# Reordering the feed-forward steps of slots 0 and 1 in a software-pipelined local-attention and feed-forward stage

## The reference, cut to what matters

```python
def local_attention(q, k, v):        # 16 heads of 64, windows of 32 that look one window back
    ...
    sim = jnp.where(mask, -jnp.finfo(sim.dtype).max, sim)
    attn = jax.nn.softmax(sim, -1)
    out = jnp.einsum('bhwij,bhwje->bhwie', attn, bv2)
...
def attn_layer(x, Wqkv, qs, ksc, Wo):
    ...
    q = l2norm(q) * qs
    k = l2norm(k) * ksc
    q = q * cos * scale + rotate_half(q) * sin * scale
    ...
    return out @ Wo
def ffn_layer(x, g, bln, W1, b1, W2, b2):
    xn = (x - mu) / jnp.sqrt(var + 1e-05) * g + bln
    hg = xn @ W1 + b1
    a, gate = jnp.split(hg, 2, -1)
    return a * jax.nn.gelu(gate, approximate=False) @ W2 + b2
for i in range(DEPTH):               # DEPTH = 6
    x = attn_layer(shift_tokens(x), ...) + x
    x = ffn_layer(shift_tokens(x), ...) + x
```

## Time and profile before

| | |
|---|---|
| median of three runs | 2726.36 us |
| the profiled execution's own time | 2725.75 us |
| its span, first to last instruction | 2723.9 us |
| mean granted TensorE clock | 0.926 of full |
| PE busy | 2409.4 us, 88% of the span |
| DVE busy | 1616.5 us, 59% |
| ACT busy | 1235.0 us, 45% |
| POOL busy | 1033.6 us, 38% |
| the stage's part of the span | about 753 to 1911 us |
| in 861 to 1885 us (1024 us): PE, DVE, ACT, POOL busy | 967.5, 826.2, 681.1, 798.4 us |
| granted clock in 861 to 1885 us | 1.00 |

### The profile page before, as it was taken

How to read it: one execution, slowest core, us unless ns; L and a number is a source line. 1 busy time by engine, 2 the same in 40 slices (tenths; PEclk the granted TensorE clock), 3 DMA queues, 4 the chain that set the end, 5 groups by cost and what they waited for, 6 DMA issues and landing times. The chain is left out here.

```text
span 2723.9 us, 46399 instructions
## 1 busy us (share of the span) xinstructions
PE 2409.4 (88%) x16011; PEld 1423.7 (52%) x16011; DVE 1616.5 (59%) x3815; ACT 1235.0 (45%) x3220; POOL 1033.6 (38%) x901
## 2 busy tenths in 40 slices
PE   5989998699679999999999999998698996996998
PEld 2446666355435555565656556565356443554443
DVE  3544544475378887888788878885463213573233
ACT  1324452155246666666666666665151111362221
POOL 2010000101188877777777878774100002000000
PEclk7989998798789999999999999999796897797999
DMA  1110000000010000000000000000000000000010
GB/s 59 25 27 1 1 1 1 16 3 2 13 39 5 21 17 14 13 17 25 9 10 25 9 14 21 14 4 1 16 3 16 23 23 12 13 2 24 23 35 19
DMA packets 45344, 41.97 MB, mean 15 GB/s; under 512 B 7421, under 2 KB 35749, under 8 KB 45108
## 3 DMA queue, kind: packets, MB, share of 16 engines
q1 hardware_dynamic: 42612, 36.59, 4.6%
q10 hardware_dynamic: 2496, 2.36, 0.4%
HBM read 33.36 MB, written 0.52 MB: 12 GB/s over the span
## 5 line engine op out<-in xcount | busy, mean ns | idle before, releaser
L3286 POOL TENSOR_TENSOR l1fb_p<-l1fb_p,l1fb_rden 128x640 f32<-128x640 f32 x192 | 240.4, 1252 | 218.6 <-DVE l1fb_rden L3353 218.6
L3278 POOL TENSOR_TENSOR l1fb_rinv<-l1fb_ssq,neghalf 128x8 f32<-128x8 f32 x192 | 319.1, 1662 | 8.5 <-DVE l1fb_ssq L3343 8.4
L3482 PE MATMUL ps<-l1fb_wqkv,l1fb_xs 128*128 128x512 f32 x576 | 298.3, 628 | 9.1 <-DVE l1fb_xs L3309 4.3
L3438 ACT ACTIVATE l1fb_p<-ps,l1fb_shift 128x128 f32<-128x128 f32 (+1 forms) x768 | 282.6, 392 | 0.3
L3280 POOL TENSOR_TENSOR l1fb_qk<-l1fb_qk,l1fb_rinv 128x512 f32<-128x512 f32 x192 | 206.6, 1076 | 15.0
L3445 ACT ACTIVATE l1fb_pT<-ps 128x512 f32<-128x512 f32 x192 | 114.7, 597 | 191.8 <-PE ps L3534 191.8
L3419 ACT ACTIVATE l1fb_sq<-ps 128x512 f32<-128x512 f32 x192 | 114.9, 598 | 169.8 <-PE ps L3482 166.0
L3348 DVE TENSOR_REDUCE l1fb_shift<-ps 128x4 f32<-128x640 f32 x192 | 157.1, 818 | 50.9 <-PE ps L3512 48.9
L3438 ACT ACTIVATION_READ_ACCUMULATOR l1fb_p<-ps,l1fb_shift 128x1 f32 x768 | 168.2, 219 | 0.0
L3534 PE MATMUL ps<-ident,l1fb_p 128*128 128x128 f32 x768 | 125.8, 286 | 41.0 <-ACT l1fb_g L3454 28.6
L3512 PE MATMUL ps<-l1fb_kT,l1fb_qT 64*128 64x128 f32 (+1 forms) x1536 | 147.3, 310 | 0.0
(11 more groups left out here) (708 smaller groups left out, 5425.6 us busy)
## 6 DMA issues: line engine op xcount, KB each, us to landing
l1fb_wqkv<-in_L_ffn_Wqkv SPq DMA_DIRECT2D x24, 256.0 KB, 2.7
l3f_w<-in_L_ffn_W SPq DMA_DIRECT2D x21, 256.0 KB, 3.1
l2f_w<-in_L_ffn_W SPq DMA_DIRECT2D x16, 256.0 KB, 3.1
l1fb_wqkv<-in_L_ffn_Wqkv SPq DMA_DIRECT2D x6, 512.0 KB, 4.1
l1fb_wo<-in_L_ffn_Wo SPq DMA_DIRECT2D x6, 512.0 KB, 4.3
l1fb_w<-in_L_ffn_W SPq DMA_DIRECT2D x6, 341.0 KB, 2.9
l1fb_w<-in_L_ffn_W SPq DMA_DIRECT2D x6, 128.0 KB
x_tok<-in_x SPq DMA_DIRECT2D x1, 512.0 KB
```

The lines of the kernel that those rows point to most:

```text
L3278: nc.gpsimd.tensor_tensor(w.rinv[:, u, :], w.ssq[:, u, :], chip.neghalf[:, 0:8], ALU.pow).then_inc(*w.unit_norm.end(f"rinv{u}"))
L3286: nc.gpsimd.tensor_tensor(p, p, w.rden[:, c, :, :].rearrange("p j q -> p (j q)").unsqueeze(2).to_broadcast([P, 2 * QT, SEEN]), ALU.mult)\
L3438: last = nc.scalar.activation(w.p[:, c % 4, j, q, 0:hi - lo], ps[:, SCORE_BANK(c) + j, lo:hi], ACT.Exp, bias=w.shift[:, c, j, q:q + 1], ac ...
L3482: nc.tensor.matmul(ps[:, PROJ_BANK(u), :], w.xs[:, x.odd, q * P:(q + 1) * P], w.wqkv[:, col:col + 512], start=True, stop=True)\
```

## The change

Three of the four strings change; no step is added or taken away, and every wait stays as it is. In slots 0 and 1 TensorE's queue has `gate2'` ahead of `V6'` and `value2'` ahead of `V7'`. ScalarE's queue has the three gelus ahead of the exponentials `X0`. VectorE's queue has `inv0` behind `att6'` and `max1` in place of ahead of them, and `g2'` ahead of the rotation `r0`. GpSimd's string stays.

```diff
-PE_PLAN = """S0 T6' t4' gate01' V6' gate2'    S1 T7' t5' p0 value01' V7' value2' p1    S2 T0 t6' y2' V0 p2    S3 T1 t7' y1 V1 p3
+PE_PLAN = """S0 T6' t4' gate01' gate2' V6'    S1 T7' t5' p0 value01' value2' V7' p1    S2 T0 t6' y2' V0 p2    S3 T1 t7' y1 V1 p3
...
-DVE_PLAN = """inv7' att5' max0 edge6' r7' tab    inv0 att6' max1 edge7' g0' g1' r0 g2'  inv1 att7' max2 edge0 x2' r1  inv2 att0 max3 edge1 r2 x1
+DVE_PLAN = """inv7' att5' max0 edge6' r7' tab    att6' max1 inv0 edge7' g0' g1' g2' r0  inv1 att7' max2 edge0 x2' r1  inv2 att0 max3 edge1 r2 x1
...
-ACT_PLAN = """c6' e4' X0 gelu0' gelu1' gelu2'    c7' e5' q0 X1 q1    c0 e6' X2 q2    c1 e7' X3 q3
+ACT_PLAN = """c6' e4' gelu0' gelu1' gelu2' X0    c7' e5' q0 X1 q1    c0 e6' X2 q2    c1 e7' X3 q3
```

## The result

The changed kernel takes **2735.21 us** (median of seven runs, 2730.09 to 2740.71) against 2726.36 before (seven runs, 2724.94 to 2728.76). The ratio is 1.0034, with a 95% interval from 1.0023 to 1.0045: slower by a third of a per cent. The forecast was 2730.2, within 0.2%; its range, 2722 to 2737.5, holds the time. The mechanism came as forecast, the sum was too small: +3.8 against +8.9. I had named the change "the same", with 5.5 us as the bound; by that bound it is slower, for which I had given 0.24.

The account below looks back on a forecast made before the run. The prediction took TensorE's idle gaps in `l1_ffn` as the bound. Its terms, +2.1 us for 21 units and +1.7 for the others, made +3.8 on 2726.36: 2730.2 us, range 2722 to 2737.5.

Parts of the forecast that it names:

- The waits: TensorE, each unit: waits of T7' and T0 go, 1.97 us; waits of 0.94 (value2') and 1.13 (t6') come.
- ScalarE's chain: ScalarE: load, gelus, second load, X0 ending at 963.40, then c7' and e5'; value2' starts at 964.42, waiting 0.94.
- rival 2: ScalarE ahead of gelu0': table load waits for the gates, +0.37 us a unit, 2735.9 us; chance 0.10.
- Behind `value2'` on TensorE: TensorE: value2', V7', p1 and S2 take 3.39 us, so T0 is reached at 967.81 and t6' at 968.30.
- The collision: Slot 1: GpSimd's n7' product gets the port ahead of VectorE's clamp; t6' at 969.43, without a lock 968.96.
- Rivals 1 and 3: Port: 1, VectorE's clamp first, -0.17 a unit, 2724.5, chance 0.14; 3, no collision, -0.37 a unit, 2720.3, chance 0.06.
- Rival 4: GpSimd's power also holds the port, delaying VectorE's addition: +0.51 us a unit, 2738.8 us; chance 0.03.
- Rival 5: TensorE: both old waits go and nothing replaces them, -1.97 us a unit, 2686.7 us; chance 0.03.
- the wait for `g2'`: TensorE at T0: this wait goes; had it been alone, it was worth 0.6 us.
- the +0.10 a unit: t6' on TensorE moves from 969.33 to 969.43 in each repeating unit; times 21, +2.1 us.
- Single units: Units outside the repeating pattern: unit 0 +0.85, unit 23 +1.54, unit 24 about -0.74 us; together +1.7.
- my own case: The forecast itself, +3.8 us to 2730.2 us, called the same; chance 0.58, with 0.08 for exceeding 5.5 us.

Follow-up runs that it names:

- e5: Changed kernel with GpSimd's n7' ahead of s0 and VectorE's tab moved from ahead of att6' to behind max1: 2715.22 us.
- e2: Changed kernel with VectorE's g2' put back behind the rotation r0: 2723.72 us.
- e7: Kernel before with the gelus ahead of X0, inv0 behind max1, n7' ahead of s0 and tab behind max1: 2710.01 us.
- e3: Kernel before with only TensorE's new order and g2' ahead of r0; ScalarE and inv0 as before: 2734.59 us.

## Why the prediction was right, and where its sum was short

- **The waits**: those that go, as forecast, `T7'` in 22 of 23 units, `g2'` in all. Those that come, 0.89 and 0.85 by the brackets, make 1.74 in a unit, inside the 1.6 to 2.4 that I had named.
- **ScalarE's chain**: the load did not wait for the gates, so rival 2 is refuted. Measured from the start of `S0` (955.33 here), `X0` begins 6.73 later and `value2'` starts 9.31 later; I had 9.30 (964.42 less 955.12, where `S0` starts in the unit of the earlier trace rows).
- **Behind `value2'` on TensorE** I was short by 0.21, without harm: `T0` starts 12.90 behind `S0` (968.23), not 12.69. `V7'` follows `value2'` after 0.60, where I had taken the 0.50 from `value2'` to `p1`, and `S2` follows `p1` after 0.96 instead of 0.86. `t6'` waits for VectorE anyway: it could have started at 968.72 and starts 1.02 later, where I had 1.13. (The bracket's 0.85 counts from the modelled end of `T0`.)
- **The collision**: the product started at 12.74, as worked out, GpSimd won, and the clamp and `att7'` took what the earlier trace rows had. Rivals 1 and 3 are refuted by these rows. Rival 4 as well: the power, L3278, runs from 966.34 to 967.99 and the addition begun inside it, at 967.68, takes its 0.68. e5 and e2 show the price by taking it away: 0.84 us a unit, about 0.5 of it for the collision and the rest for the late product.
- **Rival 5**, the gain of 1.97 a unit, failed because both chains were there; even e7, with the collision out of the way, gets 0.87 a unit. My sentence that the wait for `g2'`, alone, was worth 0.6 was wrong too: e3 takes it away alone and gains 0.04, since `att7'` ended only 0.15 ahead of `t6'`.
- **The term that was mis-sized** is the +0.10 a unit. It was +0.25. The step is "`g2'` can start when `value2'` is done (0.66), at 965.12": I let 0.04 pass between the end of the values on TensorE and the product on VectorE, 0.70 from start to start. It took 0.79 (964.64 to 965.43, and 962.91 to 963.70 in e5). Everything behind it, rotation, addition, `att7'`, `t6'`, is late by that same 0.10: `t6'` at 14.41 instead of 14.31. The trace of before had the longer one for this kind of unit: `value01'`, 963.83 and 1.03 long, and the product at 965.00, 0.14 behind its end. Unit 23, where nothing is projected or rotated in slot 1, has the short one: 0.70 from `value2'` to `g2'` in the kernel before (1858.40 to 1859.10), and the same in after although `value2'` waited there for 1.75:

```profile
1864.48 0.66 PE L3598 MATMUL ps<-l1fb_diff,l1fb_w 128*85 128x256 f32 x2 [1.75 <-ACT l1fb_qT L3424]
...
1865.18 0.48 DVE L3400 SCALAR_TENSOR_TENSOR l1fb_g<-ps,l1fb_col,l1fb_g 85x256 f32<-85x256 f32 x1 [0.34 <-PE ps L3598]
```

  So the wait ahead of `value2'` is not what makes it longer; what does stays open.
- Another 0.05 lies behind `t6'`: to `y2'` it was 0.44 us before (969.33 to 969.77) and is 0.49 now (969.74 to 970.23), and I had stopped counting at `t6'`. Twenty units then gave 5.0 us instead of the 2.1 for 21.
- **Single units**: unit 23, from one `y2'` to the next, is longer by 1.55 and 1.7 us in the two profiles of after (forecast +1.54), unit 24 shorter by 0.79 (forecast 0.74). Unit 25, which had no term, is longer by 0.5 in the mean. Unit 0's +0.85 can't be told: the part before unit 3 varies by 4 us with the clock.
- **Not in the sum at all**: the loop turns, some 1.4 us more in after, in two profiles of each kernel; whether the change brings them isn't shown.
- Together: 5.0 (period), 1.4 (turns), 1.3 (units 23 to 25: 92.5 us in before, 93.8 in after, means of two profiles each) make 7.7 of the 8.9 us; the last 1.2 is within what single profiles differ by.

With 5.0 in place of 2.1 the sum would have been +6.7, over the bound of 5.5 us; I had given 0.08 of my own case to going over it. It is partly luck that the range held the time. Its upper end, 2737.5, was there for rival 2's 2735.9, and rival 2 did not come; 2.9 us of the shortfall of 5.1 are the mis-sized term, the rest are turns, unit 25 and what no profile explains.

## What to carry to other kernels

When a step is moved past others, look on each queue for what it now falls beside, not only for what waits behind it: a product moved ahead of a rotation cost 0.49 us a unit here, and one swap on GpSimd, a queue that the change didn't touch, was worth 0.84. Before pricing a wait, look how close the next thing stands that the same step needs: a wait of 0.6 us was worth 0.04. Carry a chain to the last step that repeats (here `y2'`, not `t6'`), and take the time from one engine's end to the next engine's start from a unit of the kind that repeats, since a tenth of a microsecond is multiplied by the repetitions. Compare kernels by the period of their undisturbed units, which repeats to 0.03 us, and take two profiles before reading anything into the rest.

## What the runs showed of the hardware

- VectorE's slow-down beside GpSimd is not confined to large operations: six small products of SBUF tiles took 1.02 us alone and 2.12 beside one GpSimd addition, which itself went from 1.27 to 1.39. A clamp of 128x8 took 0.17 alone and 1.01 beside GpSimd's product. A power of 1.65 us on GpSimd did not slow an addition begun inside it (0.68), as the earlier trace rows had it.
- The Trainium skill, SBUF — State Buffer, section "SBUF: two separate sides", has a GpSimd operation exclude a VectorE operation that has two SBUF inputs or runs in a two-port mode, and the other way round. The tables, with two inputs, agree. The clamp has one input, so it would have to be in such a mode, which no trace shows; its 1.01 us agree with an exclusion. The power, which by the section's wording would hold the port for its whole length, does not agree.
- The step that follows `t6'` on TensorE starts 0.49 us behind it when `t6'` starts apart from `T0`, and 0.44 when `t6'` follows `T0` directly. `T7'` shows no such difference: `t5'` comes 0.50 behind it after a wait of 1.25 us (962.04 to 962.54 in before) and after none (960.93 to 961.43 in after).
- Shortly behind a gap of TensorE of 1.24 to 1.95 us, at a loop turn or at a wait inside a unit, the granted clock can fall to its lower level for a few microseconds. Whether it does changes between executions of one kernel; it cost a turn about 1 us and a plain unit 1.7.
